# Kept exponentials of a fused attention kernel: their transfers issued from ScalarE's queue, two behind each of eight exponentials, and the kept tiles laid out by query block

## The reference, cut to what matters

```
qkv = _qz_ring(heads + rx_theta)              # 16 heads of 8
q = jnp.transpose(qkv, (0, 2, 1, 3))
scores = jnp.einsum('bhsd,bhtd->bhst', q, q) / np.sqrt(D)
attn = jax.nn.softmax(scores, axis=-1)
ctx = jnp.einsum('bhst,bhtd->bhsd', attn, q)
```

## Time and profile before

| | |
|---|---|
| median of the timed runs | 7771.48 us (3 runs, 7758.5 to 7775.35) |
| span of the profiled execution | 7878.3 us |
| PE busy | 6921.9 us, 88% |
| ACT busy | 6811.0 us, 86% |
| DVE busy | 4954.8 us, 63% |
| POOL busy | 1244.3 us, 16% |
| exponentials into the ring | 4192, mean 1604 ns |
| exponentials into the kept tiles | 672, mean 1567 ns |
| shuffle transfers | 3584 of 128 KB, all issued by SP |
| DMA packets | 1744564, 1080.93 MB, of which 1645632 under 2 KB |

### The profile page before, as it was taken

How to read it: one execution, slowest core, us unless ns; L and a number is a source line. 1 busy time by engine, 2 the same in 40 slices (tenths; PEclk the granted TensorE clock), 3 DMA queues, 4 the chain that set the end, 5 groups by cost and what they waited for, 6 DMA issues and landing times. The chain is left out here.

```text
span 7878.3 us, 154169 instructions
## 1 busy us (share of the span) xinstructions
PE 6921.9 (88%) x58691; PEld 1859.1 (24%) x58691; DVE 4954.8 (63%) x12688; ACT 6811.0 (86%) x5455; POOL 1244.3 (16%) x1165
## 2 busy tenths in 40 slices
PE   4555799999999999999999999999999999999987
PEld 1444121111121222222221212222222212222224
DVE  5566555555555777777676767777775545454763
ACT  1222799999999999999999999999999999999971
POOL 1553111111111112111221111121210000000000
PEclk8777899999999999999999999999999999999997
DMA  6776575757566556656564545554643333232338
GB/s 214 208 210 185 125 167 138 171 137 166 141 159 147 147 135 169 154 131 157 124 144 112 138 115 132 120 136 113 145 117 77 98 74 92 69 98 64 99 98 265
DMA packets 1744564, 1080.93 MB, mean 137 GB/s; under 512 B 347914, under 2 KB 1645632, under 8 KB 1742828
## 3 DMA queue, kind: packets, MB, share of 16 engines
q1 hardware_dynamic: 1650972, 767.00, 40.2%
q0 software_dynamic: 92880, 304.42, 13.9%
HBM read 410.43 MB, written 190.83 MB: 76 GB/s over the span
## 5 line engine op out<-in xcount | busy, mean ns | idle before, releaser
L1255 ACT ACTIVATE e<-sc 128x1536 f32<-128x1536 f32 x4192 | 5715.2, 1604 | 193.2 <-PE sc L1157 121.7
L1189 PE MATMUL acc<-e,v_cur 128*9 128x512 f32 x25152 | 3341.7, 599 | 45.5 <-DVE acc_sb L1092 44.4
L1157 PE MATMUL sc<-b_unit,a_cur 32*128 32x512 f16 x14592 | 1916.7, 388 | 358.3 <-ACT e L1255 277.2
L1157 PEld LDWEIGHTS sc<-b_unit,a_cur 32*128 32x128 f16 x14592 | 472.6, 91 | 3826.3 <-ACT e L1255 2890.3
L1151 DVE STREAM_TRANSPOSE e_turned<-e_turned 128x1024 f32<-128x1024 f32 x896 | 1060.7, 1221 | 147.9 <-DMA e_turned<-e_kept 114.8
L1255 ACT ACTIVATE e_kept<-sc 128x1536 f32<-128x1536 f32 x672 | 960.6, 1567 | 63.0 <-PE sc L1157 32.1
L757 POOL DMA_INDIRECT room<-taps,idx_st x432 | 520.4, 1205 | 2109.0 <-ACT e L1255 890.2
L757 POOL DMA_INDIRECT corners<-taps,idx_st x441 | 435.1, 987 | 2052.3 <-ACT e L1255 1563.5
L1189 PE MATMUL acc<-e_kept,v_cur 128*9 128x512 f32 x4032 | 715.0, 611 | 0.0
L1189 PEld LDWEIGHTS acc<-e,v_cur 128*9 128x9 f32 x25152 | 394.3, 88 | 797.9 <-issue 730.8
L1180 PE MATMUL acc<-e_turned,v_cur 128*9 128x256 f32 x7168 | 472.2, 381 | 0.0
(11 more groups left out here) (421 smaller groups left out, 5222.5 us busy)
## 6 DMA issues: line engine op xcount, KB each, us to landing
e_turned<-e_kept SPq DMA_DIRECT2D x3584, 128.0 KB
taps<-conv_vals SPq DMA_DIRECT2D x256, 288.0 KB
taps<-cf_tapped SPq DMA_DIRECT2D x128, 288.0 KB
ew<-in_ew SPq DMA_DIRECT2D x12, 1024.0 KB, 7.8
ew<-in_ew SPq DMA_DIRECT2D x48, 256.0 KB, 6.8
x_ch<-in_x SPq DMA_DIRECT2D x4, 2048.0 KB, 12.6
qn<-q SPq DMA_DIRECT2D x64, 128.0 KB
ctx<-ctx_t SPq DMA_DIRECT2D x128, 64.0 KB
```

The source lines that it names most:

```text
L1157: last = self.nc.tensor.matmul(self.sc[k % self.SC][:, i, :], self.a[rows, t * P:(t + 1) * P], self.bst[u % 2][rows, :], start=True, stop= ...
L1189: last = self.nc.tensor.matmul(self.acc[32 * h:32 * h + self.E1, :], self.v[:, t, h, :], src, start=(i == 0), stop=(i == self.UNIT - 1))
L1255: self.nc.scalar.activation(out, self.sc[k % self.SC][:], ACT.Exp, scale=1.0 / HD ** 0.5).then_inc(self.exp_done, 1)
```

## The change

The 16 transfers of a half are issued on ScalarE's queue. `shuffle_sp` and all its calls go; `shuffle_act` issues two of the 16 and is called behind eight exponentials, those of steps k0 + 3 to k0 + 10 where k0 is the half's first kept step. The two waits that SP had stand before the first pair. `e_kept` is laid out by blocks of 128 queries: for each of four blocks, nine slabs of 128 elements, so that the source of a transfer is one run of 8 x 128 elements in a partition. The kept exponentials write, and the matmuls from kept tiles read, in four pieces of 128 columns. The other orders of SP, the order of VectorE and `PLACES` stay as they are.

```diff
-    SHUFFLES = 16
+    SHUFFLES, ISSUES = 16, 8
...
-        self.kept = sb("e_kept", [P, 9, CHUNK])
+        self.kept = sb("e_kept", [P, 9 * CHUNK])
+        self.kept_by = self.kept[:].rearrange("p (c s x) -> p s c x", c=4, s=9)
...
-    def shuffle_sp(self, sp, qd, u, half):
-        done = qd * self.QUAD_STEPS + (self.plan.halves[u, half] + 3 + self.SC)
-        used = self.plan.last_turned(u, half) + 1 if u else self.plan.last_turned(UNITS - 1, half) + 1 - UNITS * self.UNIT
-        sp.wait_ge(self.pv_done, qd * (UNITS * self.UNIT) + (self.PV_START + used))
-        sp.sem_inc(self.r.passed, 1)
-        sp.wait_ge(self.exp_done, done)
-        for a in range(4):
-            for c in range(4):
-                dst = self.turned[32 * c:32 * c + 32, a, half, :]
-                src = self.kept[32 * a:32 * a + 32, 0:self.KEPT, c * P:(c + 1) * P]
-                sp.dma_start(dst.rearrange("p (s x) -> p s x", x=P), src).then_inc(self.shuffled[half], 16)
+    def shuffle_act(self, act, qd, u, half, part):
+        if part == 0:
+            used = self.plan.last_turned(u, half) + 1 if u else self.plan.last_turned(UNITS - 1, half) + 1 - UNITS * self.UNIT
+            act.wait_ge(self.pv_done, qd * (UNITS * self.UNIT) + (self.PV_START + used))
+            act.sem_inc(self.r.passed, 1)
+            act.wait_ge(self.exp_done, qd * self.QUAD_STEPS + (self.plan.halves[u, half] + 3 + self.SC))
+        for at in range(part * self.SHUFFLES // self.ISSUES, (part + 1) * self.SHUFFLES // self.ISSUES):
+            a, c = divmod(at, 4)
+            src = self.kept[32 * a:32 * a + 32, c * 9 * P:c * 9 * P + self.KEPT * P]
+            act.dma_start(self.turned[32 * c:32 * c + 32, a, half, :], src).then_inc(self.shuffled[half], 16)
...
-                    src = self.kept[:, self.WIDE * plan.kept_step[k][2] + at, :]
+                    src = self.kept_by[:, self.WIDE * plan.kept_step[k][2] + at]
...
+        issues = {k0 + 3 + i: (u, half, i) for (u, half), k0 in plan.halves.items() for i in range(self.ISSUES)}
         for k in range(self.QUAD_STEPS):
...
-                out = self.kept[:, self.WIDE * i:self.WIDE * (i + 1), :]
+                out, src = self.kept_by[:, self.WIDE * i:self.WIDE * (i + 1)], self.sc[k % self.SC][:].rearrange("p s (c x) -> p s c x", c=4)
             else:
-                out = self.e[plan.slot[k]][:]
-            self.nc.scalar.activation(out, self.sc[k % self.SC][:], ACT.Exp,
-                                      scale=1.0 / HD ** 0.5).then_inc(self.exp_done, 1)
+                out, src = self.e[plan.slot[k]][:], self.sc[k % self.SC][:]
+            self.nc.scalar.activation(out, src, ACT.Exp, scale=1.0 / HD ** 0.5).then_inc(self.exp_done, 1)
+            if k in issues:
+                self.shuffle_act(act, qd, *issues[k])
...
-                at.shuffle_sp(sp, qd, 2 * p, 1)
```

More of the change, by code:

```diff
@@ L1695, in conv_quad @@
                 if first and p == 0:
-                    at.shuffle_sp(sp, qd, 0, 0)
                     conv.rows_sp(sp, LEAD + 1, 0)
@@ L1701, in conv_quad @@
                     at.store_ctx(sp, qd, 2 * p - 1)
-                if not (first and p == 0):
-                    at.shuffle_sp(sp, qd, 2 * p, 0)
                 conv.load_sp(sp, n + LEAD + 1)
@@ L1728, in conv_quad @@
                 if p < QPAIRS - 1:
-                    at.shuffle_sp(sp, qd, 2 * p + 1, 0)
                     if first and p == 0:
@@ L1733, in conv_quad @@
                         conv.rows_sp(sp, n + LEAD + 2, 0)
-                    at.shuffle_sp(sp, qd, 2 * p + 1, 1)
                 conv.store_sp(sp, n + LEAD)
@@ L1754, in ffn_quad @@
                     at.store_ctx(sp, qd, u - 1)
-                if u < UNITS - 1:
-                    at.shuffle_sp(sp, qd, u, 0)
                 if u in with_ffn:
                     store_gate(m0 + with_ffn.index(u))
-                if u < UNITS - 1:
-                    at.shuffle_sp(sp, qd, u, 1)
                 if u in with_ffn:
@@ L1772, in last_quad @@
             store_gate(FFN_PAIRS)
-            for half in range(2):
-                at.shuffle_sp(sp, qd, 0, half)
             for u in range(1, UNITS):
```

## The result

The changed kernel takes 8018.0 us in the median (8012.8 to 8028.8, four runs) beside 7772.9 for the kernel before on the same chip: ratio 1.0321, 95% interval [1.0307, 1.0336], 3.2% slower. The forecast was 7855, 1.1% slower; its own range was 7800 to 7930, and the range for 8 chances in 10 was 7735 to 8060. The sign and the wide range held; the time lies 163 us above the forecast and 88 above its own range, nearest to the third rival's 7980. The profiled execution spans 8011.9 us.

What follows compares the result with a forecast made beforehand. The prediction took ScalarE's exponentials, 1.346 us apiece, to bound the stage. Waits -20, pairs +78 and collisions +25 made +83 us on 7771.5: 7855 us, 1.1% slower; own range 7800 to 7930, 8 in 10 7735 to 8060.

Steps and rivals of the forecast that it cites:

- the third rival: Transfer issues on ScalarE's queue stay at 0.62 us or collide with SP's bursts: 226 us or so, less 20, 7980; chance 0.20.
- ScalarE bounds the stage: From 780 to 7624 us ScalarE is busy 6585 of 6844 us; only what shifts an exponential's start counts.
- the 107: Profiled span 7878.3 us against timed median 7771.5, 107 less; this difference was carried over unchanged.
- Gain of 20 us from waits that go: ScalarE's 19.9 us of waits for kept transfers, 13.7 in the first quad, go: 20 us gained, between 10 and 30.
- Rival 2: Issues hidden, but 14 of 21 us of ScalarE stalls put down to no engine come again: 7765, no change; chance 0.16.
- Layout at nothing: Kept exponentials and matmuls working in four pieces cost nothing, at most 34 us.
- its shorter form: One contiguous 4 KB run per partition takes 35 ns off an issue's lowest 585: 0.55 us.
- Pairs, 78 us: Two issues behind each of eight exponentials on ScalarE delay them 0.35 us a half: 78 us, bounds 0 and 226.
- Rival 1: All issues on ScalarE hidden at 0.33 to 0.48 us each, deciding at 0.485: 7751 us, faster; chance 0.27.
- rival 4: ScalarE's queue does not run on under an exponential: 1792 pairs at about 1.2 us, 2150 us, near 9900; chance 0.04.
- Collisions, 25 us: ScalarE's issues meeting SP's other issues: 25 us taken of 180 us of possible waiting.
- 180 us of such waiting: Possible waiting if issues on the two queues hold each other up: 3584 x 0.10 x 0.5 us.

Runs made afterwards that it cites:

- the layout alone: Kernel before with only the kept tiles' new layout, SP still issuing all 16 transfers of a half: 7744.4 us, ratio 0.9966 to the kernel before.
- The run that eased the pairs to the cadence: Changed kernel with a half's sixteen issues spread over ten exponentials, the 5th to the 14th, as four single issues and six pairs: 7969.5 us.
- eight on each: New layout; against the changed kernel, ScalarE issues eight of a half's sixteen transfers, one behind each of eight exponentials, SP the other eight at once: 7693.0 us.
- the 2 MB run: Changed kernel plus one 2 MB DRAM-to-DRAM transfer issued by SP in each half, released by the same exponential as the first pair: 8983.2 us.
- sixteen tiny ones: Changed kernel plus sixteen transfers of 32 partitions of 32 B issued by SP in each half, released by the first pair's exponential: 7981.1 us.

## Why the forecast held in sign and missed in size

- **ScalarE bounds the stage, and what delays an exponential counts.** Right. TensorE and VectorE execute the same instructions; 210 of the 245 us lie between the first and the last exponential. The comparison with the profile before is rough, because that execution was 107 us above its runs, and 73 of these lie ahead of the first exponential (780.4 us, 707.3 in the layout alone), so carrying the 107 over unchanged was a guess that did no harm. Against the layout alone, whose profile matches its runs (span 7750.7), the stage is 263 us longer, of 274.
- **Gain of 20 us from waits that go.** Right in the main. The 13.7 us went, and the wait for kept transfers fell from 19.9 to 7.8, so 12 of the 20 us show. The run with the first half alone on ScalarE gained 22, of which the wait explains 12.9. Rival 2's stall of 21 us is not there, but neither is it in the layout alone, so its absence tells nothing of ScalarE's longer stream.
- **Layout at nothing.** Kept matmuls 605 ns, kept exponentials 1526: no cost, as said. But it gains 23 us on SP, and 157 with pairs on ScalarE. The forecast used its shorter form only as the 35 ns off the issue; that is the right place, and SP's row shows it too (622 to 592).
- **Pairs, 78 us: the mechanism right, the size half of it.** Issue estimated at 0.55, measured 0.567 over a pair, and the reason held: no issue of a 32-partition transfer came under 507 ns. Rival 1's condition of 0.485 us an issue was not met, and rival 4 falls too. The first pair was forecast 0.21 to 0.35 us late. In the median the exponential behind it starts 0.11 late, but ends only 0.01 late, since the queue is some 0.1 us ahead of ScalarE when the pairs begin (lengths of 1.54 before the first pair, 1.45 behind it), which the forecast left out. Counted by ends, the medians of the eight steps exceed 1.343 us by 0.01, 0.08, 0.02, 0.02, 0, 0, 0.01 and 0.01, together 0.15 us a half, 34 us over 224 halves. (Counted by starts over 1.33, as the steps were read above, it would be 0.34 and 76; that is too much, because it takes the early hand-over for lost time.) The run that eased the pairs to the cadence in every median step won 49 us.
- **Collisions, 25 us: the step that failed.** 274 - 34 = 240 us, and with the pairs eased to the cadence the loss was still 225. Taking every issue against the median of its place in the half, ScalarE's issues were stretched by 286 us in all. The forecast had 180 us of such waiting in hand and wrote off all but 25, because "with 0 to 1 us of room in each step most of it is covered". Its own sum left no room: 1.30 us of issues and hand-over in 1.346. With pairs nearly all of the stretch reached the exponentials; with single issues (eight on each) 5 of 77 us did. The 180 itself was not far off for what it counts: 145 us of the stretch fall on issues beside one of SP's. The other 141 fall on issues beside none, for which the forecast had no term. Rival 3, with a chance of 0.20, had the collisions as real waits, and its sign, issues on ScalarE longer when SP's bursts run, is what the trace shows.
- **What SP does earlier: left out.** SP's other issues were taken as strewn over the stage, a tenth of it, but 170 of 256 tap stores and 27 of 62 columns loads fell into the pairs' steps, because the transfers that had stood ahead of them in SP's queue were the very ones taken away. Holding them back gave 114 us. The size of one collision was taken as 0.5 us; it is 0.42 beside a tap store and 1.05 beside a columns load. The forecast counted what SP gains by what leaves its queue, and not what SP would then do earlier.
- **What remains, 126 us** (240 - 114), lies in all quads: with ScalarE's pairs from quad 8 on only, 66 us for 112 halves, 0.59 a half, of which the medians by ends are 0.01. It is the tail once more, and mostly the issues that stand beside none of SP's, 237 of 3010 above 700 ns: their 141 us are still 150 with the tap stores held back. What stretches them was not isolated. From 1 us before their start to 0.5 us after it the DMA engines were busy 86% of the time, and 76% around the shorter ones. Together with the 2 MB run this points at transfers in flight, but no run takes them away.

The Trainium skill's "Perfetto Trace Analysis" (section DMA Instruction — HWDGE (DVE, Sync)) has the descriptor generator (DGE), which two sequencers share, locked for exclusive use by an issue. The runs agree in part: issues stretch each other (eight of SP's take 8.33 us beside ScalarE's), but sixteen tiny ones take 10.78 us beside pairs that fill most of the same time, so the whole recorded length of an issue is not exclusive. "DMA: Bandwidth & Descriptors" (section Issuing engines are not separate DMA queues) calls the time to initiate a DMA usually small against the DMA itself. Here it was not small against what counts: 519 and 614 ns in a cadence of 1.34 us went with a loss of 274 us.

## What to carry to other kernels

Count what an issue takes against the room between two instructions of the bounding engine, and leave room for the issues that take longer than the median: one issue of 0.52 us in 1.33 cost nothing that shows, two of 1.17 in all cost 274 us, 114 of them through what moved up on SP. If a sum says that something just fits, price its tail at full, not as covered. Before work is moved off a queue, ask what stood behind it there, at what moment that will now run, and beside what. And splitting transfers between an idle queue and a busy one beat giving them all to either (7693 us beside 7744 and 8018).

## What was not expected of the hardware

- Issues from one queue take longer beside those from another, the more so with pieces and with bytes in flight (means, ScalarE's issues): 1033 ns beside a store of 576 pieces and 288 KB, 743 beside 576 pieces and 18 KB, 641 beside 32 pieces of 32 B, 616 beside none; with 2 MB more in flight, 864 beside none.
- ScalarE's issue of one and the same form takes 515 ns as the first of a pair (578 in the second pair of a half) and 614 as the second. No run tells why.
- Where both queues issue the kept transfers, it is SP's that grow (592 to 769 ns in the median), ScalarE's stay at 515 in the median.
